# Input bias, maxima shift and setup of a fused convolution-attention-transformer kernel: who does them, and when

## The chip, the cores and the metric
One core of a Trainium2 chip runs the whole program. The metric is the device time of one execution in microseconds (us). Engines: PE (TensorE, matmul), PEld (its weight loads), DVE (VectorE), ACT (ScalarE), POOL (GpSimd), SP (SyncE, which here only issues DMAs). PE's clock has two levels, 1.2 and 2.4 GHz; the profile gives the granted one as 0.5 or 1.00.

## The reference
The input x has 32 images of 128 channels by 1024 pixels. For each image:

```
h    = group_norm(x)                                   # 32 groups of 4 channels
q,k,v = qkv_w @ h + qkv_b                              # over 1024 pixels
x1   = x + proj_w @ (v @ softmax(q^T k / sqrt(128))) + proj_b     # "global attention"
t    = x1 as 1024 tokens of 128
a    = window_attention(ln(t))                         # windows of 32 tokens, 8 heads of 16
m    = ln(ln(t) + a) * g1 + b1                         # transformer layer
m2   = ln(m + relu(m @ w1 + b1) @ w2 + b2) * g2 + b2
t2   = t + m2
out  = t2 + fp8_round(ln(t2)) @ fp8_round(kernel) + bias
```

Everything is fp32 in and out. The kernel writes most fp32 products as three products of 16-bit halves (high and low).

## The kernel before
An image passes through two stages. In the first (global attention) `gn0`, `gn1`, `gn2` make the group norm; `qg`, `kg`, `vg` project it (two halves of 512 columns each); 16 steps `max` multiply high halves of q and k and DVE takes each row's maximum (`cm`); `maxima` (line 684 on) reduces them per half to four maxima per partition, splits these into a bf16 high part and a rest in `cparts`; PE turns `cparts` (`shift`, line 914), DVE spreads the turned eight rows over [8 x 512] by a product with the selector `sel` (line 700), and each of the 16 score steps `st` starts its sum with one matmul of 512 columns, minus ones by this `shift` tile (line 927), before three products of halves. ACT takes the exponential, and `pv` multiplies by v, with the row sum in an extra column. `turn_x` transposes the image's own x on PE in two halves, and DVE adds proj_b as a row when it takes it out of PSUM into `xt` (line 678); `pv`'s last step adds that (line 716). In the second stage (two halves of 512 tokens each) come `ln_in`, `turn_in`, `k`, `q`, `v`, `score0/1`, `prob0/1`, `turn_p0/1`, `pv0/1`, `out`, `norm_mid`, `turn_mid`, `up0..3`, `down`, `norm_out`, `ln_q`, `quant`, `turn_q`, `ffn`.

The order of steps on each engine is written out by hand in `PROGRAM`: a word such as `max:5@4-` is step `max`, number 5, PSUM bank 4, of the image before this iteration's (one minus sign less or more is one image later or earlier). Each engine loops over the images in that order; steps wait for each other by semaphores, and a step that takes a PSUM bank also waits until its last tenant was read out. So PE has one fixed queue of work, and a late reader on DVE or ACT stops it.

Ahead of the loop stands a setup. SP issues the load of x and then 26 loads of weights and vectors that all count on one semaphore, `weights_in`. DVE waits for all of them (line 599), then makes halves of the weights and folds biases in a chain of 37 linked steps (`link`, each waiting for the last); PE waits for all 37 before the first projection. POOL makes constants, takes its part of the first group norm (`gn2`), and then clears three large tiles, `v32`, `kbd`, `ptbd`, with one memset each (line 367).

Of the kernel before, what the change touches and what calls it, by code (L numbers as in the profile page):

```python
# [25 lines left out]
P = 128  # L26
# [21 lines left out]
        max:1@0- vg:1@5- max:2@4- max:3@3- pv0:0@1-- max:4@2- max:5@4- turn_in:1@0-- pv1:0-- max:6@5- max:7@3-  # L48
        k:1@0-- out:0@4-- v:1@5-- max:8@0- q:1@3-- turn_x:0@2- shift:0@4- max:9@1- max:10@5- st:0@0- max:11@1-
        turn_mid:0@3-- pv:0- score0:1@4-- score1:1@2-- up0:0@0-- st:1@5- st:2@1- up1:0@3-- turn_x:1@4- max:12@5-  # L50
        up2:0@2-- up3:0@3-- pv:1- max:13@0- down:0@2-- st:3@0- max:14@3- max:15@5- pv0:1@1-- pv1:1-- pv:2- st:4@0-
        out:1@2-- st:5@5- st:6@0- pv:3- pv:4- gn1:0@0 shift:1@3- st:7@1- pv:5- turn_mid:1@3-- pv:6- pv:7- up0:1@2--
        up1:1@1-- up2:1@0-- up3:1@4-- st:8@3- down:1@5-- st:9@2- st:10@5- turn_in:0@2- pv:8- st:11@3- k:0@0- pv:9-
        st:12@2- q:0@1- pv:10- st:13@3- pv:11- st:14@2- gn2:0@3 turn_q:0@5-- st:15@3- pv:12- pv:13- score0:0@1-
        score1:0@0- v:0@2- pv:14- qg:0@4 kg:0@5 pv:15- vg:0@0 turn_q:1@2-- kg:1@3 qg:1@1 ffn:0@5-- max:0@5 ffn:1@2--""",
    "dve": """
        prob1:0-- kg:0- pv:15-- turn_p0:0-- ln_in:1-- qg:0- turn_p1:0-- max:0- kg:1- qg:1- max:1- max:2- max:3-
        max:4- max:5- turn_in:1-- max:6- pv1:0-- max:7- k:1-- out:0-- maxima:0- max:8- shift:0- max:9- q:1--
        turn_x:0- max:10- max:11- turn_mid:0-- score0:1-- score1:1-- prob0:1-- prob1:1-- turn_p0:1-- turn_x:1-
        turn_p1:1-- gn0:0 max:12- max:13- down:0-- max:14- max:15- pv1:1-- out:1-- maxima:1- shift:1- gn1:0  # L60
        turn_mid:1-- ln_q:0-- pv:7- ln_in:0- quant:0-- down:1-- turn_in:0- k:0- ln_q:1-- q:0- gn2:0 quant:1--
        score0:0- score1:0- prob0:0-""",
    "act": """
        vg:1- turn_in:1-- pv1:0-- k:1-- q:1-- v:1-- norm_mid:0-- st:0- turn_mid:0-- score0:1-- up0:0-- st:1-
        score1:1-- st:2- up1:0-- load_x:0 up2:0-- up3:0-- st:3- pv1:1-- st:4- norm_out:0-- st:5- st:6- norm_mid:1--
        st:7- turn_mid:1-- up0:1-- up1:1-- up2:1-- up3:1-- quant:0-- st:8- norm_in:0- st:9- turn_in:0- st:10-
        norm_out:1-- k:0- st:11- q:0- st:12- st:13- quant:1-- gn2:0 st:14- st:15- turn_q:0-- v:0- score0:0-
        score1:0- kg:0 turn_q:1-- qg:0 ffn:0-- qg:1 kg:1 vg:0 ffn:1-- norm_in:1-""",
    "pool": """
        prob1:0-- ln_in:1-- out:0-- norm_mid:0-- prob0:1-- prob1:1-- bias_out:1-- keep:0-- down:0-- out:1--  # L70
        norm_out:0-- norm_mid:1-- ln_q:0-- keep:1-- ln_in:0- quant:0-- down:1-- norm_out:1-- ln_q:1-- gn2:0
        quant:1-- prob0:0- bias_out:0-""",
# [72 lines left out]
def build(nc, a, out, images=IMAGES):  # L145
    ctx = ExitStack()
    with ctx:
# [23 lines left out]
        BO, RG1, RB1, RB2, RG2, RBL2, PROJR = range(7)  # L171
        rows = sb("rows", [P, 7, P])
# [6 lines left out]
        sel = sb("sel", [2 * HT, HT, P])  # L179
        minus1 = sb("minus1", [P, P], BF16)  # L180
# [19 lines left out]
        chi = sb("chi", [P, HT], BF16)  # L200
        cparts = sb("cparts", [P, P])
        shift = sb("shift", [P, 2, HT, P], BF16)
# [25 lines left out]
        wraw = xt[:].rearrange("p a b c -> p (a b) c")  # L228
        w1raw, kraw = e[:, 0, 0, :], et[:, 0, 0, 0:P]
        ones = p32[:, 0, 0:P]  # L230
        vb_full = p32[:, 1, 0:2 * P].rearrange("p (a b) -> p a b", b=P)
# [5 lines left out]
        def tiles(ap):  # L237
# [3 lines left out]
        s = {n: sem(n) for n in """weights_in const_made const_mask setup_dve setup_mm  # L241
            x_in gn_stats gn_mv gn_mm gn_mean gn_diff gn_var gn_veps gn_pow gn_scale gn_neg gn_coef h32_made h_hi h_lo
# [51 lines left out]
        def _(sp):  # L294
            def load(dst, src):
                sp.dma_start(dst, src).then_inc(s["weights_in"], 16)

            def prologue():
                sp.dma_start(x_sb[:, :], a["x"][0]).then_inc(s["x_in"], 16)
                load(wraw[:, QG:QG + 2, :].rearrange("p a b -> p (a b)"), a["qkv_w_t"][:, 0:2 * P])  # L300
                load(wraw[:, VG, :], a["v_w"])
                load(wraw[:, PROJ, :], a["proj_w_t"])
                load(wraw[:, Q:Q + 3, :].rearrange("p a b -> p (a b)"), a["in_w_t"])
                load(wraw[:, OUT, :], a["out_w_t"])
                load(w1raw, a["w1_t"])
                load(w2[:], a["w2_t"].rearrange("(t p) d -> p t d", p=P))
                load(kraw, a["kernel"])
                with nc.allow_non_contiguous_dma("short vectors, once"):
                    for at, width, name in ((QGB, 3, "qkv_b"), (PROJB, 1, "proj_b"), (GNW, 1, "gn_w"), (GNB, 1, "gn_b"),
                                            (QB, 3, "in_b"), (LN1B, 1, "ln1_b"), (FFNB, 1, "ffn_b"), (B1, FT, "b1"),  # L310
                                            (LN1G, 1, "ln1_g")):
                        load(cols[:, at:at + width], a[name].rearrange("(t p) -> p t", p=P))
                    load(col(S_IN), a["s_in"].partition_broadcast(P))
                    load(col(S_K), a["s_k"].partition_broadcast(P))
                for at, name in ((BO, "out_b"), (RG1, "ln1_g"), (RB1, "ln1_b"), (RB2, "b2"), (RG2, "ln2_g"),
                                 (RBL2, "ln2_b"), (PROJR, "proj_b")):
                    load(rows[:, at, :], a[name].partition_broadcast(P))
# [23 lines left out]
        def _(pool):  # L341
            g = nc.gpsimd

            def prologue():
# [10 lines left out]
                g.affine_select(out=sel[:], in_=sel[:], compare_op=ALU.not_equal, fill=1.0, base=0,  # L355
# [5 lines left out]
                g.affine_select(out=sel[:], in_=sel[:], compare_op=ALU.not_equal, fill=1.0, base=-HT,  # L361
                                pattern=[[-1, HT], [0, P]], channel_multiplier=1).then_inc(s["const_mask"], 1)
                for tile, value in ((cparts[:], 0.0), (minus1[:], -1.0), (vg32[:], 1.0), (ones, 1.0), (shift[:], 0.0)):
                    g.memset(tile, value).then_inc(s["const_made"], 1)
                gn2(None, 0, 0)
                for tile in (v32, kbd, ptbd):
                    g.memset(tile[:], 0.0).then_inc(s["const_made"], 1)
# [81 lines left out]
        def _(act):  # L449
# [22 lines left out]

            def normalise(dst, src, k):
# [20 lines left out]
            def vg(kind, img, c):  # L494
                act.wait_ge(s["vg_mm"], upto(img, c + 1, per=2))
                if isinstance(img, int) and img == 0 and c == 0:
                    act.wait_ge(s["const_made"], 10)
# [3 lines left out]
                sc.activation(vg32[:, HT * c:HT * (c + 1), 0:C], tiles(bank("vg", c)), ACT.Copy).then_inc(s["vg_made"], 1)  # L501

# [28 lines left out]
            def v(kind, img, h):  # L531
                n = 2 * img + h
                act.wait_ge(s["v_mm"], upto(n))
                if isinstance(img, int) and img == 0:
                    act.wait_ge(s["const_made"], 13)
# [31 lines left out]
            def ffn(kind, img, h):  # L567
# [3 lines left out]
                if due(value := upto(img - 1, step=16)):  # L571
# [6 lines left out]
                      "quant": normalise(z, u, 3), "load_x": load_x, "gn2": gn2, "qg": global_hi("qg", qgh, QGB), "kg": global_hi("kg", kgh, KGB), "vg": vg, "st": st,  # L578
# [7 lines left out]
        def _(dve):  # L586
# [9 lines left out]
            def prologue():  # L596
                gn0(None, 0, 0)
                dve.wait_ge(s["weights_in"], 16 * 26)
                dve.wait_ge(s["const_made"], 10)
                dve.wait_ge(s["const_mask"], 6)  # L600
# [500 lines left out]
```

## Time and profile before

| | us |
|---|---|
| median of 3 runs (lowest to highest) | 2459.72 (2457.88 to 2463.32) |
| the profiled execution | 2464.32 |
| its span, first to last instruction | 2462.6 |
| PE busy in the span | 2184.8 (89%) |
| DVE, ACT, POOL busy | 1878.0 (76%), 1380.6 (56%), 1224.1 (50%) |

The busy shares are means over the start, the steady loop and the end. A matmul's busy time in the profile contains its latency, so matmuls that follow each other overlap, and PE's share is not its share of peak.

### The profile page before, as it was taken

The numbers are of one execution on the slowest core, as the hardware profiler recorded it, in microseconds if no ns is written. First come the engines' busy times: TensorE is split into PE (matmuls) and PEld (weight loads), VectorE is DVE, ScalarE is ACT, GpSimd is POOL, SyncE is SP. The second block draws the span as 40 slices with busy tenths as digits, with TensorE's granted clock in tenths as the row PEclk, the third lists the DMA queues.
The fourth block names the chain that finished last, engine by engine and source line by source line (L and its number), as shares of the span: only waits on it lengthen the run. The fifth ranks groups of instructions, "written<-read, shape, count | busy, mean of one in ns | idle before, by whom it ended". The sixth has DMA issues, their size and how long they took to land.

```text
span 2462.6 us, 63216 instructions
## 1 busy us (share of the span) xinstructions
PE 2184.8 (89%) x21489; PEld 1606.4 (65%) x21710; DVE 1878.0 (76%) x5861; ACT 1380.6 (56%) x2721; POOL 1224.1 (50%) x1303
## 2 busy tenths in 40 slices
PE   1798899999999999999999999999999999999984
PEld 0566667766667766666776666676666677666663
DVE  5488777778777778887777888777887777788753
ACT  0355566555565555556655556665555655555653
POOL 5044455544455645455554545555544555444544
PEclk9999999999999999999999999999999999999997
DMA  1011111111101111110111111111111011111110
GB/s 34 14 31 44 43 28 38 26 38 43 43 26 39 27 40 38 43 43 26 38 26 40 41 43 38 30 38 26 38 43 43 26 38 26 41 40 43 29 31 19
DMA packets 76238, 86.15 MB, mean 35 GB/s; under 512 B 20640, under 2 KB 55584, under 8 KB 76192
## 3 DMA queue, kind: packets, MB, share of 16 engines
q1 hardware_dynamic: 62512, 52.51, 9.3%
q10 hardware_dynamic: 13680, 33.04, 3.9%
q8 instruction: 28, 0.46, 0.1%
q14 instruction: 18, 0.15, 0.0%
HBM read 18.36 MB, written 16.78 MB: 14 GB/s over the span
## 4 chain that ended last, share of the span: by engine, by line
PE 63%; DVE 11%; issue 6%; ACT 4%; DMA 4%; SPq 1%; ACTq 1%; POOL 1%; DVEq 0%; POOLq 0%
PE ps L944 16%; PE ps L851 9%; PE ps L852 8%; PE ps L853 8%; PE ps L1037 6%; PE ps L1006 5%; DMA x_sb<-in_x 3%; PE ps L911 3%; PE ps L988 3%; PE ps L954 2%; PE ps L927 2%; DVE cm L682 2%; DVE stats L723 1%; DVE y L794 1%; ACT o_sb L573 1%
## 5 line engine op out<-in xcount | busy, mean ns | idle before, releaser
L382 POOL TENSOR_TENSOR rstd<-veps,halfpow 128x4 f32<-128x4 f32 x256 | 266.7, 1042 | 816.0 <-DVE veps L731 814.9
L944 PEld LDWEIGHTS ps<-vg,p 128*128 128x128 f32 x4096 | 511.1, 192 | 49.0 <-issue 12.1
L944 PE MATMUL ps<-vg,p 128*128 128x129 f32 x4096 | 533.2, 277 | 0.6 <-ACT p L508 0.6
L508 ACT ACTIVATE p<-ps 128x512 f32<-128x512 f32 x512 | 294.4, 587 | 260.6 <-PE ps L853 260.6
L682 DVE TENSOR_REDUCE cm<-ps 128x1 f32<-128x512 f32 x512 | 330.4, 676 | 16.9 <-PE ps L911 16.7
L1037 PEld LDWEIGHTS ps<-w,hid 128*128 128x128 f32 x2048 | 235.2, 192 | 17.9 <-ACT hid L560 12.8
L1037 PE MATMUL ps<-w,hid 128*128 128x128 f32 x2048 | 242.3, 277 | 1.8 <-ACT hid L560 1.7
L851 PE MATMUL ps<-qgh,kgh 128*128 128x512 f16 x512 | 194.5, 380 | 42.9 <-DVE shift L700 19.9
L911 PE MATMUL ps<-kgh,qgh 128*128 128x512 f16 x512 | 173.9, 392 | 61.5 <-ACT vg L501 37.4
L560 ACT ACTIVATE hid<-ps,cols 128x512 f32<-128x512 f32 x256 | 170.7, 686 | 72.3 <-PE ps L853 72.3
L853 PE MATMUL ps<-qgh,kgl 128*128 128x512 f16 x512 | 194.5, 380 | 0.0
L852 PE MATMUL ps<-qgl,kgh 128*128 128x512 f16 x512 | 194.5, 380 | 0.0
L416 POOL TENSOR_TENSOR e<-e,srec 128x512 f32<-128x512 f32 x128 | 134.3, 1050 | 119.8 <-DVE srec L774 119.7
L482 ACT ACTIVATE y<-y,nshift,rstd 128x128 f32<-128x128 f32 x256 | 105.6, 483 | 77.6 <-POOL nshift L389 77.6
L1006 PE MATMUL ps<-ptbd,v 128*32 128x128 f32 x4096 | 137.0, 281 | 11.5 <-DMA ptbd<-et 11.5
L1006 PEld LDWEIGHTS ps<-ptbd,v 128*32 128x32 f32 x4096 | 109.8, 113 | 47.6 <-issue 29.0
L482 ACT ACTIVATE z<-u,nshift,rstd 128x128 f32<-128x128 f32 x256 | 105.1, 481 | 60.5 <-POOL nshift L389 60.5
L741 DVE TENSOR_TENSOR xl<-ps,xh 128x512 f16<-128x512 f32 x128 | 87.8, 686 | 62.0 <-ACT xh L516 59.5
L546 ACT ACTIVATE e<-e 128x512 f32<-128x512 f32 x128 | 80.6, 630 | 92.9 <-DVE e L764 92.9
L482 ACT ACTIVATE y<-t,nshift,rstd 128x128 f32<-128x128 f32 x256 | 105.5, 482 | 42.8 <-POOL nshift L389 24.0
L516 ACT ACTIVATE xh<-ps 128x512 f16<-128x512 f32 x128 | 76.4, 597 | 73.8 <-PE ps L954 73.8
L927 PE MATMUL ps<-shift,minus 128*128 128x512 bf16 x291 | 111.1, 382 | 5.0 <-DVE cm L682 4.8
(188 smaller groups left out, 5439.9 us busy)
## 6 DMA issues: line engine op xcount, KB each, us to landing
ptbd<-et SPq DMA_DIRECT2D x512, 64.0 KB, 2.0
kbd<-kk SPq DMA_DIRECT2D x512, 32.0 KB, 2.0
out_y<-o_sb ACTq DMA_DIRECT2D x64, 256.0 KB, 2.3
x_sb<-in_x ACTq DMA_DIRECT2D x31, 512.0 KB, 3.3
x_sb<-in_x SPq DMA_DIRECT2D x1, 512.0 KB, 3.5
e<-in_w_t SPq DMA_DIRECT2D x1, 256.0 KB, 3.6
w<-in_w_t SPq DMA_DIRECT2D x1, 256.0 KB, 3.4
xt<-in_in_w_t SPq DMA_DIRECT2D x1, 192.0 KB, 2.8
```

What stands on the lines that cost most here:

```text
L382: g.tensor_tensor(rstd[:, k, h, :], veps[:, k, h, :], halfpow[:], ALU.pow).then_inc(s[f"ln_pow{k}"], 1)
L482: last = sc.activation(dst[:, h, P * j:P * (j + 1)] if dst is z else dst[:, h, j, :], src[:, h, j, :], ACT.Identity, bias=nshift[:, k, h, ...
L508: sc.activation(p32[:, c % PRING, :], bank("st", c), ACT.Exp, scale=C ** -0.5).then_inc(s["p_made"], 1)
L560: sc.activation(hid[:, f, :], bank(f"up{f}", h), ACT.Relu, bias=col(B1F + f)).then_inc(s["hid_made"], 1)
L682: v_.reduce_max(cm[:, c // 2, c % 2:c % 2 + 1], bank("max", c), X).then_inc(s["max_out"], 1)
L851: mm(dst, lhi, rhi, start=first, stop=False, **kw)
L852: mm(dst, lhi, rlo, start=False, stop=False, **kw)
L853: return mm(dst, llo, rhi, start=False, stop=last, **kw)
L911: mm(bank("max", c), qgh[:, P * (c // 2):P * (c // 2 + 1)], kgh[:, HALF * (c % 2):HALF * (c % 2 + 1)], start=True, stop=True).then_inc(s[" ...
L944: last = mm(ps[:, b, at:at + PVW], p32[:, c % PRING, part], vg32[:, j, :], start=j == 0 and q % 2 == 0, stop=j == MT - 1, skip_group_check ...
L1006: last = mm(ps[WIN * two:WIN * (two + 1), BANK["pv0", h], P * j:P * (j + 1)], v32[:, h, odd, j, WIN * two:WIN * (two + 1)], ptbd[:, h, j, ...
L1037: last = mm(bank("down", h)[:, part], hid[:, f, part], w2[:, f, :], start=f == 0, stop=f == FT - 1)
```

## The change
Six edits, made together:

- turn_x: ACT adds proj_b to x_sb in place, per channel, in one step `bias_x`, after the group norm has read x; PE's transposes wait for it, and ACT, not DVE, copies them into `xt` (two copies of 512 columns). The folded bias of v (v's bias times proj_w) is a column now and not a row.
- shift: `cparts` is bf16, its transpose is a bf16 one, ACT, not DVE, copies the turned eight rows ([8 x 128]), and the spreading over 512 columns is done by PE: each `st` starts with four matmuls of 128 columns with four stationary tiles of a bf16 selector that holds -1. The separate tile `chi` is gone.
- the setup's loads: seven (qkv_w, v_w, proj_w, qkv_b, gn_w, gn_b, proj_b) come first on a semaphore of their own, `first_in`; the other 18 follow.
- the setup's DVE chain: seven steps come before the loop (halves of q's and k's weights, the product v times proj and its bias); the rest runs on DVE as the end of `maxima:0` of the first image, and PE's part at the end of its first `shift` step. The first `pv` waits for the steps that read PSUM, the first `turn_in` for all.
- POOL clears `v32`, `kbd`, `ptbd` in 26 pieces in place of three.
- `PROGRAM` is a new order on all engines, with other banks. Among others `out:0` and `gn0` come after `maxima` and no longer before it.

```diff
+        max:1@1- max:2@2- max:3@0- vg:1@5- turn_in:1@3-- pv0:0@1-- max:4@2- max:5@5- k:1@4-- max:6@0- pv1:0--
+        max:7@3- turn_x:0@4- v:1@5-- out:0@2-- q:1@1-- shift:0@0- turn_x:1@3- max:8@2- st:0@4- max:9@0- st:1@3-
...
-        for tile in (v32, kbd, ptbd):
-            g.memset(tile[:], 0.0).then_inc(s["const_made"], 1)
+        for h in range(2):
+            g.memset(v32[:, h], 0.0).then_inc(s["const_made"], 1)
+            for head in range(HEADS):
+                g.memset(kbd[:, h, head], 0.0).then_inc(s["const_made"], 1)
+            for j in range(HT):
+                g.memset(ptbd[:, h, j], 0.0).then_inc(s["const_made"], 1)
...
+    def bias_x(kind, img, _):
+        act.wait_ge(s["h32_made"], upto(img))
+        sc.activation(x_sb[:], x_sb[:], ACT.Identity, bias=col(PROJB)).then_inc(s["x_bias"], 1)
+    def turn_x(kind, img, c):
+        sc.activation(xt[:, c], tiles(bank("turn_x", c)), ACT.Copy).then_inc(s["xt_made"], 1)
+    def make_shift(kind, img, c):
+        sc.activation(shift[0:2 * HT, c, :], bank("shift", c)[0:2 * HT, 0:P // 2].bitcast(BF16),
+                      ACT.Copy).then_inc(s["shift_made"], 1)
...
     def prologue():                                    # DVE
         gn0(None, 0, 0)
-        dve.wait_ge(s["weights_in"], 16 * 26)
...
         gn1(None, 0, 0)
+        dve.wait_ge(s["first_in"], 16 * 7)
+        halves(QG)
+        halves(KG)
         gn2(None, 0, 0)
         dve.wait_ge(s["setup_mm"], 1)
...
+    def setup_rest():                                  # DVE, at the end of maxima:0 of image 0
+        dve.wait_ge(s["weights_in"], 16 * 18)
+        link(v_.tensor_scalar(vb_full, ones, col(VB), None, ALU.mult))
+        halves(Q)
+        halves(K)
+        dve.wait_ge(s["rest_mm"], 1)
...
     def st(kind, img, c):                              # PE
-        mm(bank("st", c), minus1[:], shift[:, h].rearrange("p a b -> p (a b)"), start=True, stop=False)
+        for q in range(HT):
+            mm(bank("st", c)[:, P * q:P * (q + 1)], sel[:, q, :], shift[:, h, :], start=q == 0, stop=False,
+               skip_group_check=True)
         three(bank("st", c), kgh[:, keys], kgl[:, keys], qgh[:, queries], qgl[:, queries],
-              first=False).then_inc(s["st_mm"], 1)
+              first=False, skip_group_check=True).then_inc(s["st_mm"], 1)
```

## Rows read from the trace of the kernel before

**Rows 1.** Windows: length, busy of PE, PEld, DVE, ACT, POOL, clock, DMA.
```profile
1354.50:1426.90 72.40, 67.22 (x673) 49.63 (x679) 57.65 (x182) 43.06 (x85) 37.47 (x41) 1.00 0.14 36
1358.70:1391.70 33.00, 28.53 (x328) 19.62 (x323) 31.45 (x76) 20.25 (x39) 15.57 (x15) 1.00 0.19 52
```
**Rows 2.** Timeline of PE, one iteration: start, length, idle before and releaser.
```profile
1354.56 0.28 PE L879 MATMUL ps<-gtmp,group_mean 128*128 128x1 f32 x2
...
1426.94 0.28 PE L879 MATMUL ps<-gtmp,group_mean 128*128 128x1 f32 x2
```
**Rows 3.** Waits of PE in that iteration: total, times, longest.
```profile
PE ps L917 <- DVE cparts L695: 1.3, 1, 1.3
PE ps L911 <- ACT vg L501: 1.2, 1, 1.2
PE ps L911 <- ACT o_sb L573: 0.8, 1, 0.8
PE ps L851 <- DVE shift L700: 0.6, 1, 0.6
```
**Rows 4.** Timeline of DVE in that iteration.
```profile
1377.10 0.68 DVE L794 TENSOR_TENSOR y<-ps,y 128x512 f32<-128x512 f32 x1
...
1379.28 0.15 DVE L687 TENSOR_REDUCE cmax<-cm 128x4 f32<-128x8 f32 x1
...
1392.71 0.69 DVE L639 BATCH_NORM_STATS2 gst<-x_sb 128x6 f32<-128x512 f32 x1 [1.00 <-DMA x_sb<-in_x]
```
**Rows 5.** Groups by form, 1000 to 2200 us: busy, mean ns, idle before.
```profile
L927 PEld LDWEIGHTS ps<-shift,minus 128*128 128x128 bf16 x261 | 26.1, 100 | 35.6 <-DVE cm L682 18.2 <-DVE w L805 6.6 <-DVE gtmp L655 2.9
...
L678 DVE TENSOR_TENSOR xt<-ps,rows 128x512 f32<-128x512 f32 x34 | 22.5, 661 | 0.0
L700 DVE TENSOR_TENSOR shift<-ps,sel 8x512 bf16<-8x512 f32 x33 | 22.2, 674 | 15.6 <-PE ps L917 15.6
...
L501 ACT ACTIVATE vg<-ps 128x512 f32<-128x512 f32 x34 | 20.0, 587 | 0.0
L461 ACT ACTIVATE hh<-x_sb,gtmp 128x1024 f16<-128x1024 f32 x16 | 19.6, 1227 | 0.0
```
**Rows 6.** Timeline of PE: a 512-column bf16 matmul.
```profile
1387.09 0.38 PE L927 MATMUL ps<-shift,minus 128*128 128x512 bf16 x1
```
**Rows 7.** Timeline: four 128-column bf16 matmuls, each with its own weights.
```profile
1001.93 0.39 PE L1046 MATMUL ps<-identh,qz 128*128 128x128 bf16 x4
```
**Rows 8.** Timeline of the start, all engines; SPq is SP's issue queue.
```profile
0.80 0.40 SPq L299 DMA_DIRECT2D x_sb<-in_x  x1
...
6.59 0.43 SPq L296 DMA_DIRECT2D cols<-in_gn_b  x1
...
18.30 0.28 DVE L601 TENSOR_SCALAR p<-p,cols 128x128 f32<-128x128 f32 x1 [12.44 <-DMA rows<-in_proj_b]
...
22.64 0.16 DVE L655 TENSOR_SCALAR gtmp<-ps 128x1 f32<-128x1 f32 x1 [3.08 <-PE ps L879]
...
27.57 1.80 POOL L367 MEMSET v<- 128x2048 f32 x1
27.81 15.33 DVE L607 CAST wh<-xt 128x128 f16<-128x128 f32 x1
29.32 13.75 POOL L367 MEMSET kbd<- 128x16384 f16 x1
...
43.50 6.58 DVE L607 CAST wh<-xt 128x128 f16<-128x128 f32 x1
50.12 0.29 DVE L608 TENSOR_TENSOR wl<-xt,wh 128x128 bf16<-128x128 f32 x1
...
58.81 0.10 PEld L851 LDWEIGHTS ps<-hh,wh 128*128 128x128 f16 x1 [36.30 <-DVE kl L635]
```
**Rows 9.** DMA issues: size, us to landing.
```profile
cols<-in_gn_b SPq DMA_DIRECT2D x1, 0.5 KB, 2.3
```
**Rows 10.** Timeline of PE in the loop's first full pass.
```profile
85.20 0.61 PE L927 MATMUL ps<-shift,minus 128*128 128x512 bf16 x1 [4.79 <-DVE cm L682]
```

## What was predicted before the changed kernel ran
> **What bounds the kernel now.** I read the busy line and the 40 slices first: PE is high in all slices but the first two and the last two. So there are two questions: what one iteration of the steady loop costs, and what the start costs. For the loop I took one iteration on PE's timeline, from one image's second group-norm matmul to the next: 1426.94 - 1354.56 = 72.4 us [rows 2]; 31 such iterations make 2244 us of 2462.6. In it PE is busy 67.2 us, DVE 57.7, ACT 43.1, POOL 37.5 [rows 1], so PE bounds the loop and what can be won is its waits. The view of waits names them [rows 3]: 1.3 us for `cparts` before the transpose of the maxima, 1.2 and 0.8 at the loop's end where `max` waits for ACT's read-out, 0.6 for `shift`; with three smaller ones 4.8 us in all. They lie in or beside a stretch of 33.0 us in which DVE is busy for 31.45 [rows 1]: there DVE, not PE, sets the pace. So DVE work is dear inside this stretch and nearly free outside it. For the start the timeline says it plainly: the first projection's weights load at 58.81, after a wait of 36.3 us for the last step of DVE's chain [rows 8]. That chain waited to 18.30 for the last of 26 loads, and two of its casts took 15.33 and 6.58 us, each ending as one of POOL's large memsets does.
>
> **The start.** Issues lie (6.59 - 0.80)/12 = 0.48 us apart [rows 8], so the seventh load after x goes out at 0.8 + 7 x 0.48 = 4.2, and with 2.3 us to landing [rows 9] `first_in` is full at 6.5 (qkv_b has three columns: 7). The group norm's first half, which needs only x, is through by then. PE makes two small products and the second group-norm matmul, about 1.6 us, to 8.7. From that matmul's reader to POOL's first large memset, which starts as the low half of the normed image is made, are 27.57 - 22.64 = 4.9 us [rows 8]: 13.6. The seven DVE steps (two pairs in front of it, three behind) hide in this. So the first projection starts at about 14 in place of 58.8: **45 us earlier**, 40 if a load or a lock adds five.
>
> Not all of it stays. The rest of DVE's chain moves behind `maxima:0` of image 0. Before, from 50.12 to 58.8 [rows 8], the chain's free-running end took 8.6 us, for the same number of steps within three. Behind it on DVE stand `max:8` and all later maxima, and PE waits for their banks; PE has some 3 us of its own there (`turn_x:1`, two `st`, two `max`), so 8.6 - 3 = 5.6 us return. POOL cleared from 27.57 to the end of the second long cast at 50.08 [rows 8], 22.5 us; in 26 pieces it does so from 14 to 37, and in this time (the rest of the chain starts near 28) DVE's casts meet them. If a cast waits for one piece, half a piece of 0.87 is 0.4 us for each of about 12: +4, of which the last few fall after 37. If it doesn't get in between pieces (the cast of 27.81 outlasted the 1.80 us memset of `v` and ended with that of `kbd` at 43.1 [rows 8]), it stands until 37: +9. I take +4. The first full pass also had a 4.79 us wait of PE [rows 10]: DVE stood in `gn0` for the next x with two `max` behind it. `gn0` moves behind `maxima:1`, so this goes: -4. Sum of the start: -45 + 5.6 + 4 - 4 = -39, rounded down to **-37** for steps I can't see (bounds -28 and -44).
>
> The Trainium skill (SBUF — State Buffer, section on ports) says that the pair of ports which VectorE and GpSimd share is locked for a whole instruction. The trace agrees in that the casts end with memsets, not in that a boundary between two memsets was enough; by the rule taken to the letter pieces cost half a piece each, which is the +4 I took.
>
> **The loop, DVE and ACT.** DVE loses two `turn_x` of 661 ns, two `shift` of 674 ns [rows 5] and two small copies, 3.0 us an iteration; three of the four large ones and one copy, 2.2 us, lie in the crowded stretch. `out:0` stood before `maxima:0` and held it for 1379.28 - 1377.10 = 2.2 us [rows 4]; now it is behind. So `cparts` comes about 3 to 4 us earlier relative to the `max` steps, more than the 1.3 us that PE waits there. The `shift` link shrinks from a 674 ns DVE step queued behind a `max` to a small ACT copy of about 0.25. `gn0`'s 1.00 us wait for its DMA [rows 4] leaves the front of `max:12` too. ACT gains one [128 x 1024] Identity, 1.23 us as `hh`, two copies of 587 ns [rows 5] and two small ones: +2.9 us, to 46 of 70. Its steps that PE waits for soon (`turn_q`, `o_sb`, `kgh`, `vg`) aren't behind `bias_x`; `k:1` is, and had its result needed only six steps later.
>
> **The loop, PE.** One 512-column matmul (0.38 us busy, [rows 6]) becomes four of 128 with their own weights; four such in a row are busy 0.39 [rows 7]. So +0.01 x 16 = 0.2 us at most, and a bf16 transpose in place of an fp32 one gives back about 0.1. I take zero (bounds -0.1 and +0.3 an iteration).
>
> **The loop, the order.** I added up step durations along PE's new queue and looked at each wait by hand. Waits I still find: about 0.4 at `ffn:1` for `turn_q`, 1.4 at `max:1` (its bank is released by DVE's `qg:1`, which stands behind `ln_in`, two transposes and `qg:0`), 0.6 at `turn_mid:0`, and 1.4 in crumbs. Gone are the two for the maxima (1.3 + 0.6), the `ol` one, and half of that at the loop's end: up to 2.8 us won. Each hand-over I left out goes against this, so I take two thirds, **-1.8 us an iteration** (bounds: -3.2 and, as any order can hide a new wait of a DMA or a POOL step, +0.3), x 31 = **-56 us**. The end (the last image's second stage) I take as unchanged, +-4.
>
> **Sum.** The profiled execution took 2464.3; 2464.3 - 37 - 56 = 2371. The median of the runs lies 4.6 lower at 2459.7, from which the same sum gives 2367. I say **2369**.
>
> **Rivals.**
> 1. Only the start gains. The PE waits at the loop's end are of ACT and DVE order, not of load, and a new order can trade 1.9 us of one wait for others: iteration 72.4 as before, time 2460 - 37 = 2423. For it: each wait in [rows 3] is at most 1.3 us, about what one step placed two places too early brings back. Against: 2.2 us of DVE work leaves a stretch that has only 1.5 us of slack.
> 2. Slower by ACT. The 2.9 us land in front of `p`, and `pv` on PE waits for it; no more than four `p` tiles are open. If all of it shows, 31 x 2.9 = +90, less the start's 37: 2513. It decides from +1.2 us an iteration on. For it: `norm_mid` and `st` share that stretch of ACT. Against: ACT is busy 43 of 72, and 20 of 33 in the stretch [rows 1].
> 3. Slower by weight loads. Of four loads of 100 ns [rows 5] three are new; were they in the open between short matmuls, 0.3 x 16 x 32 = +154, less 37: 2577. Against: [rows 7]. The Trainium skill (TensorE: Matmul & The Clock Gate, "Back-to-back issue gap") speaks for a milder form: 81 ns for each 128-column matmul in a stream of load and matmul pairs and 131 for a 512-column one, by which 16 x 32 x (324 - 131) ns = +99 us; the trace has neither figure, its 128-column ones being spaced as [rows 7] shows.
> 4. The start gives less, because DVE's chain stands behind POOL's pieces until 37 and `v`'s or `kbd`'s readers wait too: start -28, time 2378 with the loop as forecast.
>
> **How the numbers follow.** Loop and start both gain: 0.72 (rival 4 is in it). Only the start: 0.17. ACT 0.05, weight loads 0.03; 0.03 for a loop that loses just what the start wins. The likeliest case itself spans 2464 - 44 - 99 = 2321 to 2423. To hold 8 in 10 the range leaves out the far low end and takes in rival 1: 2328 to 2430. With about 0.2% (5 us) as what can be told from no change: faster 0.90, same 0.02, slower 0.08.
>
> **What would show it.** First projection near 14, and DVE's chain after `maxima:0` about 10 us long with PE waiting some 6 to 10 in it. An iteration of 70.6 between second group-norm matmuls; no PE wait for `cparts` or `shift`; the 128-column selector matmuls spaced so that `st` stays near 0.86 us; the 4.79 wait gone. DVE 54.7 and ACT 46 busy an iteration. Wrong if an iteration is 72 or more, or if the largest PE wait names an ACT step behind `bias_x`, or DMA-fed `pv0`/`pv1`.

## The result, and the profile after

| | before | changed |
|---|---|---|
| median of four runs, us | 2460.10 (2457.88 to 2463.32) | 2379.01 (2369.09 to 2409.28) |
| ratio | | 0.966, 95% interval 0.961 to 0.971 |
| span of the profiled execution | 2462.6 | 2407.5 |
| to the second group-norm matmul of image 1 | 115.2 | 77.2 |
| from there to that of image 31, 30 passes | 2184.0 | 2172.4 |
| from there to the end | 163.4 | 157.9 |

The time lies 10 us from the forecast of 2369, with the sign as forecast. The runs of the changed kernel spread over 40 us, those of before over 5; the profiled one is the slowest of the four, so by their times it holds more of the long passes told below than the other three. The ratio leaves this run out, since its 2409.28 lies more than 1.5% above the fastest of its kernel.

**A pass as it should be.** The windows of the changed kernel show one iteration (length, busy of PE, PEld, DVE, ACT, POOL, clock, DMA share, GB/s), then one of 80 us:

```profile
1115.84:1185.54 69.70, 67.82 (x729) 51.49 (x728) 54.19 (x177) 45.60 (x90) 37.55 (x41) 1.00 0.14 38
291.12:371.06 79.94, 70.56 (x729) 53.24 (x727) 54.52 (x177) 45.65 (x90) 37.61 (x40) 0.94 0.13 35
```

The first row answers to [rows 1]: 69.7 us for 72.4, DVE 54.2 busy (57.7 before), ACT 45.6 (43.1 before). PE's waits in seven such passes (1046 to 1534 us; total, times, longest), all that the view lists:

```profile
PE ps L938 <- DVE qgl L704: 9.0, 7, 1.3
PE ps L929 <- DVE kk L779: 1.6, 7, 0.2
PE ps L1092 <- ACT qt L586: 1.1, 7, 0.2
```

Of the four waits of [rows 3] none is there: `cparts`, `vg`, `o_sb` and `shift` hold PE no more. One of 1.3 us stands in their place, at `max:1`. All waits together are 11.7 / 7 = 1.7 us a pass, against 4.8.

**Eight passes that aren't.** Of the 30 passes between the two matmuls 22 take 69.7 to 71.7 us, and eight take 78 to 80. PE's timeline at the end of one of them (start, length, idle before):

```profile
304.54 0.38 PE L938 MATMUL ps<-kgh,qgh 128*128 128x512 f16 x1
309.06 1.44 PE L938 MATMUL ps<-kgh,qgh 128*128 128x512 f16 x3 [4.14 <-issue]
...
312.27 0.27 PE L877 MATMUL ps<-wh,hl 128*128 128x128 f16 x1 [1.24 <-issue]
```

The releaser is "issue": the profile shows nothing that PE waited for. What PE's queue did in that time is one instruction, the branch at the loop's end. Its group in the changed kernel (line, queue, operation: ns min/median/max, first and last start), and the queue of instruction loads of that pass, then of the whole span (packets, MB, share):

```profile
L285 PEldq COMPARE_BRANCH  x28: 76/213/4896, 304.2 to 2261.8; - x28
```
```profile
q8 instruction: 9, 0.15, 0.8%
```
```profile
q8 instruction: 102, 1.67, 0.3%
```

The branch takes 0.21 us in 20 passes and 4.4 to 4.9 us in eight, the eight of 78 to 80 us. Before, the longest was 0.24 us and the queue moved 28 packets in all; now each of the eight has nine packets of 16 KB and a clean one has none. The two idle stretches, 4.14 and 1.24, are half of the 79.9 - 69.7 = 10.2 us by which this pass is longer. Most of the other half is the clock, in the windows around it:

```profile
304.10:309.10 5.00, 0.86 (x11) 0.53 (x8) 3.15 (x6) 2.82 (x6) 0.54 (x2) 0.76 0.40 109
309.10:319.00 9.90, 8.66 (x90) 5.28 (x90) 4.96 (x8) 3.00 (x5) 2.50 (x2) 0.61 0.13 31
```

PE stood for 4.1 us, and in the 10 us after it the granted clock was 0.61: most of them at 1.2 GHz. By an estimate this costs 9.9 x (1 - 0.61) = 3.9 us. Behind the other seven long branches the 10 us show 0.54 to 0.68.

**The start.** DVE and PE around the first projection and the first maxima:

```profile
13.47 0.27 PE L875 MATMUL ps<-wh,hh 128*128 128x128 f16 x1 [5.33 <-POOL hl L380]
```
```profile
26.40 10.17 DVE L720 CAST cparts<-cmax 128x4 bf16<-128x4 f32 x1
```
```profile
36.91 0.27 PE L944 MATMUL ps<-identh,cparts 128*128 128x128 bf16 x1 [12.03 <-DVE cparts L722]
...
47.65 0.61 PE L938 MATMUL ps<-kgh,qgh 128*128 128x512 f16 x1 [3.39 <-DVE cm L710]
```

The first projection runs at 13.47 in place of 58.8 [rows 8]. But the cast of four numbers per partition, the first DVE instruction of its kind after POOL began to clear, takes 10.17 us: it ends at 36.57, as POOL's last piece does (36.5). While PE waits for it, the granted clock falls, by the window from 30 to 40 us to 0.50:

```profile
30.00:40.00 10.00, 3.09 (x15) 3.12 (x16) 8.45 (x9) 0.27 (x1) 6.54 (x8) 0.50 0.00 0
```

From 40 to 50 us it is 0.67, and PE's 512-column matmuls of that time take up to 0.63 us in place of 0.38. The prediction's sum of the start has no term for the clock.

### The profile page after: what moved, and what is told of

It reads as the page before. It is cut to its first block, busy times and chain, and to the rows that moved or that the text cites. A ratio compares the mean times of both kernels' runs of the same rounds, so it can differ in the third digit from the quotient of the medians.

```text
span 2407.5 us, 66541 instructions
## 1 busy us (share of the span) xinstructions
PE 2210.5 (92%) x23246; PEld 1672.1 (69%) x23246; DVE 1757.0 (73%) x5668; ACT 1461.4 (61%) x2881; POOL 1229.0 (51%) x1325
## 3 DMA queue, kind: packets, MB, share of 16 engines
q8 instruction: 102, 1.67, 0.3%
## 4 chain that ended last, share of the span: by engine, by line
PE 66%; DVE 10%; issue 8%; ACT 6%; DMA 5%; SPq 4%; POOL 1%; ACTq 0%; DVEq 0%; POOLq 0%
PE ps L977 15%; PE ps L875 8%; PE ps L1072 8%; PE ps L877 7%; PE ps L876 7%; PE ps L1041 4%; PE ps L957 4%; PE ps L938 4%; DMA ptbd<-et 3%; PE ps L1023 3%; PE ps L989 3%; SPq L323 2%; DMA kbd<-kk 2%; SPq L330 1%; ACT y L498 1%
## 5 line engine op out<-in xcount | busy, mean ns | idle before, releaser
L977 PEld LDWEIGHTS ps<-vg,p 128*128 128x128 f32 x4096 | 503.5, 192 | 37.6 <-ACT p L529 4.6
L977 PE MATMUL ps<-vg,p 128*128 128x129 f32 x4096 | 520.6, 277 | 0.7 <-ACT p L529 0.7
L710 DVE TENSOR_REDUCE cm<-ps 128x1 f32<-128x512 f32 x512 | 335.9, 681 | 40.4 <-PE ps L938 40.2
L938 PE MATMUL ps<-kgh,qgh 128*128 128x512 f16 x512 | 183.2, 398 | 69.4 <-issue 34.8
L581 ACT ACTIVATE hid<-ps,cols 128x512 f32<-128x512 f32 x256 | 165.7, 684 | 96.3 <-PE ps L877 96.3
L957 PE MATMUL ps<-shift,sel 128*128 128x128 bf16 x2048 | 198.6, 220 | 0.0
L957 PEld LDWEIGHTS ps<-shift,sel 128*128 128x128 bf16 x2048 | 155.4, 98 | 56.7 <-ACT hid L581 2.1
L403 POOL TENSOR_TENSOR y<-y,rows 128x512 f32<-128x512 f32 x64 | 81.5, 1273 | 172.2 <-PE ps L989 172.2
L572 ACT ACTIVATE oh<-ps 128x512 f16<-128x512 f32 x64 | 38.2, 597 | 186.9 <-PE ps L1041 186.9
L938 PEld LDWEIGHTS ps<-kgh,qgh 128*128 128x128 f16 x512 | 49.3, 98 | 143.8 <-issue 99.3
```

What stands on the lines that cost most here:

```text
L581: sc.activation(hid[:, f, :], bank(f"up{f}", h), ACT.Relu, bias=col(B1F + f)).then_inc(s["hid_made"], 1)
L710: v_.reduce_max(cm[:, c // 2, c % 2:c % 2 + 1], bank("max", c), X).then_inc(s["max_out"], 1)
L938: mm(bank("max", c), qgh[:, P * (c // 2):P * (c // 2 + 1)], kgh[:, HALF * (c % 2):HALF * (c % 2 + 1)], start=True, stop=True).then_inc(s[" ...
L957: mm(bank("st", c)[:, P * q:P * (q + 1)], sel[:, q, :], shift[:, h, :], start=q == 0, stop=False, skip_group_check=True)
L977: last = mm(ps[:, b, at:at + PVW], p32[:, c % PRING, part], vg32[:, j, :], start=j == 0 and q % 2 == 0, stop=j == MT - 1, skip_group_check ...
```

## The experiments

**What makes the long passes.** PE's part of the loop grew from 1483 to 1581 instructions, counted in the traces (the trace of before shows 1476, with 671 matmuls for 678 weight loads; before_moves below, which has the same steps, shows all 1483). My theory was that none of its steps is slow, and that where the loop lies decides whether its first instructions are still held at the branch. The rivals: the number of instructions, or the short weight loads.

`pad32` and `pad96`: the changed kernel with 32 or 96 PE instructions ahead of the loop that wait for something long done.

```diff
             def prologue():
+                for _ in range(N):             # and as many behind gn2; two waits make one instruction
+                    pe.wait_ge(s["const_made"], 1)
                 gn1(None, 0, 0)
```

> The changed kernel with 32 more PE instructions ahead of the loop (waits that are already met), nothing else. In the changed kernel's trace PE's branch at the loop's end takes 0.21 us in 20 of 28 passes and 4.4 to 4.9 us in 8, and exactly in those passes the instruction queue moves nine packets of 16 KB; the passes last 78 to 80 us in place of 69.7. Theory (instruction fetch): PE's loop of 1581 instructions covers seven blocks of 256 and ends near a block's end; what was kept of the loop is lost when fetching runs past it. Counted from where the packets fall ahead of the loop, 32 more instructions make it span eight blocks: all 28 branches slow, some 250 instruction packets, time near 2330 + 28 x 9 = 2580 us, slower than the kernel before. Rival A (clock): the slow passes come from PE's clock alone, set off by the waits in the order: 0 to 10 slow passes as now, 2370 to 2410 us. Rival B: random DMA contention: the same.

> The same with 96 such instructions: by the instruction-fetch theory the loop then spans seven blocks and ends 80 instructions into its last: no slow branch, some 28 instruction packets, every pass 69.7 us, time 2367.3 less its slow passes, near 2335 us (the 96 waits cost up to 3 at the start). Rival A and B: 2370 to 2410 us with up to 10 slow passes, as the changed kernel.

Measured: pad32 2334.89 (2334.17 to 2335.68), ratio 0.947 (0.945 to 0.949); pad96 2330.62 (2326.78 to 2333.53), 0.945 (0.943 to 0.948). Neither has a long branch. pad96:

```profile
L285 PEldq COMPARE_BRANCH  x28: 76/208/234, 301.4 to 2183.8; - x28
```
```profile
q8 instruction: 30, 0.49, 0.1%
```

So position decides, and rivals A and B are out. Some 48 us (2379.0 - 2330.6; by the two ratios 2.0%, 50 us) come back with instructions that do nothing. But my count of blocks, by which 32 would make all passes slow, was wrong.

`one512`: the changed kernel with one 512-column selector matmul that reads the 128-column shift four times over; 1485 PE instructions in the loop. This kernel leaves out a part of the computation: three of the four query tiles of a half are shifted by the maxima of another tile and not by their own.

```diff
-                for q in range(HT):
-                    mm(bank("st", c)[:, P * q:P * (q + 1)], sel[:, q, :], shift[:, h, :], start=q == 0, stop=False, ...)
+                mm(bank("st", c), sel[:, 0, :], shift[:, h:h + 1, :].to_broadcast([P, HT, P]), start=True, stop=False, ...)
```

> The changed kernel with one matmul of 512 columns ahead of each score step in place of four of 128 (the shift tile read four times over; the shift subtracted is then that of another query tile, so this part of the computation is changed). PE's loop body is 96 instructions shorter. Theory: four short matmuls cost what one long one does (0 to +0.3 us a pass), and the loop no longer ends near a block's end: no slow branch, 69.4 to 69.7 us a pass, 2325 to 2340 us. Rival A (clock): slow passes stay, 2370 to 2410. The rival of the prediction by weight loads (81 ns for each short matmul): a pass shorter by 3 us, 2240.

Measured: 2326.84 (2324.02 to 2329.52), ratio 0.944 (0.942 to 0.946), no long branch, pass 69.63 against 69.70. The 48 additional matmuls and their loads cost 0.07 us a pass, where the rival by weight loads had 3.

`before_split`: the opposite direction. The kernel before, its 512-column matmul cut in four with the same minus ones; 1579 PE instructions in the loop (its trace shows 1575 to 1583 in a pass, that of split_pad 1579 in each).

```diff
-                mm(bank("st", c), minus1[:], shift[:, h].rearrange("p a b -> p (a b)"), start=True, stop=False)
+                for q in range(HT):
+                    mm(bank("st", c)[:, P * q:P * (q + 1)], minus1[:], shift[:, h, q, :], start=q == 0, stop=False, ...)
```

> The kernel before with each 512-column matmul of minus ones cut into four of 128 columns, nothing else: 96 more PE instructions in the loop (1572). Theory: 72.4 to 72.7 us a pass; the loop spans seven blocks and ends 56 instructions ahead of its last block's end, so few or no slow branches: 2460 to 2470 us. If the mere number of instructions is what counts, slow passes come as in the changed kernel: 2490 to 2540. Rival (weight loads): +3 us a pass, 2550.

Measured: 2578.97 (2563.93 to 2592.35), ratio 1.048 (1.043 to 1.053), where I expected few or no long branches: the count of blocks failed here too. Most clean passes stay at 72.4 to 72.6; 11 of 28 branches take 5.0 to 5.9 us and their passes 80 to 82.

```profile
L287 PEldq COMPARE_BRANCH  x28: 76/222/5919, 353.5 to 2410.7; - x28
```
```profile
q8 instruction: 129, 2.11, 0.4%
```

The fault is carried into a kernel that hadn't it, without one step of the change's order. `split_pad` then takes it away from there: before_split with 96 instructions of padding.

> The kernel before with its 512-column matmul cut in four (before_split, 2578.97, with 11 long branches of 28), and besides 96 PE instructions that wait for nothing ahead of the loop. If what makes the long branches is where the loop lies among the instructions, and not how many it has (1575 in both), they are gone: no branch over 0.3 us, about 28 instruction packets, every pass 72.4 to 72.5 us, and 2462 to 2472 us. If the number of instructions in the loop is what counts, the time stays at 2560 to 2590 with 10 or so long branches.

Measured: 2469.18 (2463.74 to 2476.33), ratio 1.002 (1.001 to 1.004), no long branch.

```profile
L287 PEldq COMPARE_BRANCH  x28: 76/208/246, 352.3 to 2318.3; - x28
```

The same loop with the same 1579 instructions, 110 us apart: it is the position, shown in both directions. It also prices the weight loads in the kernel before: cut and padding cost 6 us together, of which 3.0 lie ahead of the second group-norm matmul of image 1 and 3.4 in the 30 passes behind it, 0.1 a pass. Which positions are bad stays half open. Counted along the trace, good to two or three, the first branch is PE's instruction 5578 in the changed kernel and 5563 in before_split, 202 and 187 modulo 256. In the kernels without long branches the rest is 25 (split_pad), 42 (pad96 and the runs built on it), 57 (before_moves, with the PE steps of before), 74 (one512, yield_one) and 234 (pad32). Why only 8 to 11 of 28 branches are long stays open too. The Trainium skill (Runtime: NRT & Kernel Launch, "Instruction fetch mechanics") says that PE's instructions are refilled in 16 KiB blocks of 256, and that a taken branch whose target isn't held forces a fetch before execution goes on. The packets of 1.67 MB / 102 = 16.4 KB and the branches of 4.9 us agree. That the same loop is held or not by its position, and in one pass of three, the section doesn't say.

**What the start is worth.** All on pad96, against its 2330.6, since no long pass covers a few us there.

`bigmem`: three large clears again in place of 26 pieces.

```diff
-                for h in range(2):
-                    g.memset(v32[:, h], 0.0)...          # and 8 pieces of kbd, 4 of ptbd
+                for tile in (v32, kbd, ptbd):
+                    g.memset(tile[:], 0.0).then_inc(s["const_made"], 1)
```

> The same base, with POOL's 26 clears put back into three. In the base DVE's four-element cast of the maxima stands from 26.7 to 36.9, through 12 pieces, until POOL's last one ends. Theory (DVE doesn't get in between pieces, so pieces are worth nothing): the cast waits until a clear ends and DVE gets in at 29 or at 36.6 as before: start the same within 1 us or up to 1 us shorter, 2330. Rival (pieces help): start 2 to 5 us longer, 2335.

Measured: 2329.06 (2327.42 to 2330.22), ratio 0.945 (0.944 to 0.947). The pieces are worth nothing. The cast of bigmem beside its clears, then that of pad96 beside its own:

```profile
15.31 13.75 POOL L366 MEMSET kbd<- 128x16384 f16 x1
29.00 6.92 POOL L366 MEMSET ptbd<- 128x8192 f32 x1
```
```profile
26.86 9.08 DVE L716 CAST cparts<-cmax 128x4 bf16<-128x4 f32 x1
```
```profile
25.19 0.95 POOL L366 MEMSET v<- 128x1024 f32 x1
26.08 7.21 POOL L368 MEMSET kbd<- 128x1024 f16 x8
33.23 3.64 POOL L370 MEMSET ptbd<- 128x1024 f32 x4
```
```profile
26.71 10.19 DVE L720 CAST cparts<-cmax 128x4 bf16<-128x4 f32 x1
```

The cast of bigmem ends at 35.94 with the 6.92 us clear, passing over the boundary at 29.0; that of pad96 passes over eleven. In these two runs no boundary between two clears that stand in POOL's queue one behind the other lets the waiting cast in; in the kernel before, one of two did (see the part on the prediction).

`yield`: POOL stops after 13 pieces until the setup's chain is through.

```diff
                 for h in range(2):
+                    if h:
+                        pool.wait_ge(s["setup_dve"], SETUP_STEPS)
                     g.memset(v32[:, h], 0.0).then_inc(s["const_made"], 1)
```

> The same base, POOL clears the first 13 pieces (to 25.2 us) and waits for DVE's setup chain before the other 13. Theory (the 10.2 us of the cast are POOL's clears): the cast takes 0.2, DVE's chain ends near 37 in place of 47, and PE's first pass is 8 to 10 us shorter: 2321. Rival (the cast's length has another cause, or the later clears stop something else by the same time): 2331.

Measured: 2320.17 (2318.68 to 2320.51), ratio 0.941 (0.940 to 0.943). DVE and POOL in yield:

```profile
28.14 0.17 DVE L722 CAST cparts<-cmax 128x4 bf16<-128x4 f32 x1
```
```profile
22.12 3.64 POOL L372 MEMSET ptbd<- 128x1024 f32 x4
37.65 0.95 POOL L368 MEMSET v<- 128x1024 f32 x1 [11.88 <-DVE kl L669]
```

With POOL idle the same cast takes 0.17 us, and 10.4 us of the total go, about what the cast stood; 8.6 of them lie ahead of the second group-norm matmul of image 1 (68.9 for 77.6).

`onechain`: the chain's second part back in front of the loop on DVE and PE, loads and pieces as changed.

```diff
                 link(v_.tensor_tensor(col(PROJB), ps[:, 7, FT:FT + 1], col(PROJB), ALU.add))
+                setup_rest()
...
-                if isinstance(img, int) and img == 0 and c == 0:
-                    setup_rest()
```

> pad96 (2330.6 us) with all of DVE's and PE's setup steps in front of the loop again, not at the end of the first maxima; the two-part loads, the early casts of q's and k's weights and POOL's 26 pieces stay. My theory: the gain of the start comes of the first projection that no longer waits for the chain. Then the first projection waits for the last of 25 loads (about 15 us), the two setup products and a chain of some 9 us which begins before POOL's clears: it starts at 24 to 32 us in place of 13.8, PE's stop behind maxima:0 (some 12 us) goes in return, and so the time is only 2 to 12 us longer, 2333 to 2343. If one of the chain's casts is caught by POOL's pieces again, as in the kernel before, the projection waits to about 45 to 50 us and the time is 2350 to 2360. Rival: moving the chain is worth nothing, because its length comes back whole behind maxima:0 and what won was only the early end of the waiting for the loads: 2328 to 2333.

Measured: 2337.18 (2324.37 to 2339.78), ratio 0.947 (0.944 to 0.951). The first projection comes at 37.56, 24 us later than in pad96, since again one DVE step stood for POOL:

```profile
17.87 19.04 DVE L639 TENSOR_SCALAR res<-res,cols 128x128 f32<-128x128 f32 x1 [6.23 <-DMA rows<-in_ln_b]
```

It costs 6.6 us by the medians, inside my 2333 to 2343, though the first projection came in neither of my two windows, and the intervals of the two ratios overlap. In the traces the second group-norm matmul of image 1 comes 8.4 us later (85.9 for 77.6). So of the 37.7 us that the start gained to this matmul, the chain's new place gives some 8, although it moves the first projection by 24: PE's 12.0 us wait behind `maxima:0` is 1.6 here. The larger part comes of what this kernel keeps. I put it down to the loads in two parts, which is argued: no run has all loads on one semaphore again. Without the two parts gn2, and with it POOL's clears, had to wait for 26 loads; POOL was through at 50.1 [rows 8] and is at 36.9 here, and DVE's chain ends 13 us earlier (58.8, here 45.4) though undivided. The step is a TENSOR_SCALAR, so casts aren't the only kind that stands.

**What the loop is worth.** `turnx_dve`: pad96 with the two copies of `turn_x` on DVE as before, put behind `maxima:0` and `max:8`.

```diff
-        max:6- pv1:0-- max:7- maxima:0- out:0-- max:8- max:9-            # DVE's order
+        max:6- pv1:0-- max:7- maxima:0- turn_x:0- out:0-- max:8- turn_x:1- max:9-
```

> The same base, with the two turn_x copies back on DVE (two steps of 0.66 us, put behind maxima:0 and max:8), the bias left on ACT. Theory of the prediction (work on DVE in the crowded stretch is dear): 1.2 us more in that stretch, of which PE has to wait some 0.6 to 1.2: 70.3 to 70.9 a pass, 2350 to 2368. Rival (the gain of the loop came from the new order, not from the load): +0 to 0.2 us a pass, 2331 to 2337.

Measured: 2399.85 (2394.63 to 2422.35), ratio 0.973 (0.971 to 0.974). That is over my 2350 to 2368. A clean pass is 71.63, +1.9, more than the 1.3 us that the two copies take. PE's waits, 1100 to 1600 us:

```profile
PE ps L946 <- DVE qgl L704: 11.4, 7, 2.4
PE ps L965 <- DVE xt L710: 9.2, 7, 1.3
```

In a clean pass `st` now waits 1.3 us for a bank that DVE's copy gives back, `max:1` waits its 1.3 as before, and small ones (`y` of DVE and of ACT, 0.2 each) make up the rest. DVE work near the crowded stretch comes through whole and more.

Nine of the 30 passes take 73 to 76 us besides. In each of the nine, and in no other of the 30, one DVE step of 0.43 us in `quant` stands beside POOL's `hl`:

```profile
524.39 2.13 POOL L380 TENSOR_TENSOR hl<-h,hh 128x1024 f16<-128x1024 f32 x1 [2.31 <-ACT hh L464]
524.39 2.41 DVE L850 TENSOR_SCALAR expo<-expo 128x512 f32<-128x512 f32 x1
```

Here the two start within 0.02 us of each other in nearly every pass. If POOL is first, DVE's step takes 2.4 us and `max:1` waits 2.4; if DVE is first, its step takes 0.43 and `hl` 2.4. In pad96 DVE is 0.05 us or more ahead wherever the two meet, and its step always takes 0.43. So the two copies also moved DVE to the edge of a collision with POOL, and a part of the 69 us (2399.9 - 2330.6) is that.

`before_moves`: the opposite, the order without the load. The kernel before with `out:0` behind `maxima:0` and `gn0` behind `maxima:1` on DVE.

```diff
-        ... k:1-- out:0-- maxima:0- max:8- ...   gn0:0 max:12- ...   maxima:1- shift:1- gn1:0
+        ... k:1-- maxima:0- out:0-- max:8- ...   max:12- ...   maxima:1- gn0:0 shift:1- gn1:0
```

> The kernel before with two moves in DVE's order alone: out:0 behind maxima:0, gn0 behind maxima:1. If the order near the maxima makes up much of the changed kernel's 2.7 us a pass, this alone gives 0.3 to 1.0 us a pass and takes the 4.79 us wait of the first pass away: 2425 to 2450. If what won is DVE's lighter load, and the order only moves waits between steps, the pass stays within 0.3 us of 72.4 and the time is 2450 to 2468.

Measured: 2501.45 (2498.77 to 2504.66), ratio 1.016 (1.014 to 1.018): slower, which neither of my cases had. The pass is 73.6, +1.2. PE's waits, 1100 to 1600 us, of before_moves:

```profile
PE ps L927 <- DVE shift L700: 8.5, 7, 1.2
PE ps L911 <- ACT vg L501: 6.9, 6, 1.2
PE ps L874 <- DVE gmv L643: 5.9, 7, 0.8
PE ps L911 <- ACT o_sb L573: 4.7, 6, 0.8
PE ps L954 <- ACT y L482: 4.3, 7, 0.6
PE ps L911 <- ACT v L540: 4.0, 7, 0.6
```

The wait for `cparts` (1.3 a pass, [rows 3]) is gone as meant. In its place stand `shift` with 1.2 (0.6 before), `gmv` with 0.8, since `gn0` and `gn1` now come late for the group norm, and `y` and `v` with 0.6 each. Only the start gained (gn2 of image 1 at 111.3, the 4.79 us wait gone). So the two moves that I had priced as gains don't pay in the old order. Whether they do in the new one, with the lighter DVE, no run shows by itself.

`swap`: pad96 with the banks of `max:1` and `max:2` exchanged, against the one large wait left.

```diff
-        max:1@1- max:2@2- max:3@0-
+        max:1@2- max:2@1- max:3@0-
```

> The changed kernel with 96 more PE instructions ahead of the loop (as run before: no slow pass, 69.7 us a pass, 2330.6), and banks 1 and 2 exchanged between max:1 and max:2. In each pass PE waits 1.3 to 1.6 us at max:1, whose bank is read out by DVE's qg:1; bank 2 is released by qg:0, one DVE step of 0.65 earlier. Theory (this wait is set by DVE's queue, and nothing close behind it): 69.1 us a pass, 31 x 0.6 = 19 less, 2312. Rival (the next wait takes it over: vg:1 needs bank 5 from DVE's max:0, pv0 its DMA): no change, 2331.

Measured: 2332.93 (2331.74 to 2333.57), ratio 0.947 (0.945 to 0.948), pass 69.79: no gain. PE's waits in it, 1100 to 1600 us:

```profile
PE ps L942 <- DVE qgl L704: 4.9, 14, 0.5
PE ps L993 <- ACT y L498: 2.2, 7, 0.3
...
PE ps L1045 <- DVE cm L710: 1.1, 5, 0.2
```

1.3 us at one place have become 0.7 at two together, 0.3 for `y` and 0.15 for `cm`. The bank only moves the wait; my reading is that DVE's pace sets it, which this run fits and doesn't prove.

**The fastest version.** `yield_one`: the changed kernel with yield's wait and one512's matmul, without padding. It leaves out what one512 leaves out, the own maxima of three tiles in four; of the versions that compute everything yield is the fastest.

> The changed kernel with the two things that won apart: POOL stops its clears after 13 pieces until the setup's chain is done (yield, 2320.2 on the padded kernel), and one 512-column matmul for the shift in place of four of 128 (one512, 2326.8 against 2330.6). No added PE instructions: with 1485 in the loop it lies where one512 and the kernel before have no long branches. If the gains add: 2313 to 2319. If they don't, because the 3.8 us of one512 came of something in the start which yield removes too: about 2320.

Measured: 2317.49 (2315.68 to 2319.87), ratio 0.941 (0.939 to 0.942): 62 us below the changed kernel, 3 below yield, though their ratios (0.9405 and 0.9413) can't be told apart.

## Why the prediction was near, and where it was wrong

The forecast was 2369; with the long passes taken out the changed kernel is 2330.6 (pad96). So 2379 lies close to the forecast because two errors cancel: I gave the loop and the end too little by some 40 us (2369 - 2330.6), and didn't foresee a fault that costs about 48. That the number came out near is luck. By the spans, pad96 against before (2328.2, 2462.6):

| | forecast | pad96 | changed kernel's profile |
|---|---|---|---|
| start (to gn2 of image 1) | -37 | -37.7 | -38.0 |
| loop | -56 | -89.9 | -11.6 |
| end | 0 | -6.8 | -5.5 |

- **The start** came out as summed, by terms that were not. The first projection at 13.5 to 13.8 was right (14). "Half a piece for each of about 12 casts: +4" failed: the bound beside it, a cast that stands until 37, is what happened, by one cast (to 36.6). Behind it the chain's second part took 10.3 us, as said; PE waited 12.0 + 3.4 = 15.4 us, where I had 5.6 + 4. The 4.79 us wait is gone, as said. -45.3 + 15.4 - 4.8 = -34.7, and most of the rest to -38 is the shorter pass, 2.7 us, which stood in the loop's term. The low clock behind the 12.0 us wait, for which I had nothing, is within these numbers and not told apart.
- **My reading of the pair of ports** was the mistake in this. In [rows 8] the first long cast passes over the boundary at 29.3 and ends at 43.14, just behind the boundary between `kbd` and `ptbd`, whose clear stands in the same trace:

```profile
43.01 7.00 POOL L367 MEMSET ptbd<- 128x8192 f32 x1
```

  So one boundary in two had let a cast in, and I took the price by which every one does. In bigmem, pad96 and onechain no boundary let the waiting step in, and it ended with POOL's last clear; in yield, with POOL idle, it ran at once. What decides at which boundary DVE gets in stays open. The Trainium skill (SBUF — State Buffer, "Who interferes with whom") has the lock for the whole of one instruction; that a step waits through twelve of them, as the cast of pad96 does, the section doesn't say. It says also that `cast` and `tensor_scalar` can take the shared pair and `tensor_reduce` never; there the trace agrees, as the stalled steps are a CAST and a TENSOR_SCALAR, and the TENSOR_REDUCE at 26.51 of pad96, 0.2 us ahead of the cast and under the same clear, took its 0.16 us.
- **The loop** was right in its mechanism and too small: 72.4 - 69.7 = 2.7 us a pass, where I had written 2.8 and taken two thirds of it. The mis-sized term is the third that I took off for hand-overs left out. The 2.8 itself doesn't follow from the waits listed beside it: those called gone add to 1.3 + 0.6 + 0.4 + 1.0 = 3.3, and those still found to 3.8 of the 4.8, which leaves 1.0; that it came out near 2.7 is no merit of the sum. The waits that I said would go went, the one named at `max:1` stands with 1.3 (I had 1.4), `turn_q` with 0.16 (0.4), `turn_mid` has none (0.6). DVE 54.2 and ACT 45.6 busy answer to 54.7 and 46. How the 2.7 divides stays open: with the two copies back on DVE 0.8 of it is left (72.4 to 71.6), two moves of the order in the kernel before lose 1.2, and no run has the lighter DVE in the old order.
- **The matmuls**: a step `st` is 0.87 us and the shift's four matmuls 0.39; one512 gives 0.07 us a pass for them, against 4.8 by rival 3 and 16 x 193 ns = 3.1 by its milder form, the 81 and 131 ns of the Trainium skill (TensorE: Matmul & The Clock Gate, "Back-to-back issue gap"). Both are dead in this kernel; rival 2 (ACT) too, as no wait of PE names a step behind `bias_x`.
- **Rival 1** (only the start gains) is what the span of this profile nearly shows, -11.6 us over 30 passes, and yet its mechanism, waits traded for waits, wasn't there. Who reads only the sums would have taken it as right.
- **What I left out**: I counted what PE does with 48 more matmuls and 48 more loads a pass, and not what the loop's length does to its instruction supply. The trace of before had a row for it, the 28 packets of instructions against 28 branches of 0.2 us, but nothing in it that could have told on which side of the edge the new loop would fall.

## What to carry to other kernels

When a hardware loop gets longer, look first at the loop-end branch of the engine that bounds and at the packets of the instruction queue: 96 idle instructions ahead of the loop were worth 48 us here, more than the start's 38. Don't clear large tiles on POOL while DVE has a critical chain, and don't count on the boundaries between pieces: make POOL wait. If single passes of a loop are longer than the others, compare the lengths of their steps with those of a clean pass: in turnx_dve a start a few hundredths of a us behind POOL's cost 3 us. In an order written by hand, price DVE work by the stretch that it lies in, and don't price a move by the wait that it removes alone.

## What the runs showed of the hardware

- PE's loop-end branch takes 0.21 us or 4.4 to 5.9 us, the latter with nine 16 KB instruction packets and, in the changed kernel, a granted clock of 0.54 to 0.68 in the 10 us after; in 8 (changed kernel) or 11 (before_split) of 28 passes, and in none with 96 instructions more ahead of the loop.
- A DVE cast of 4 elements per partition waited 10.19 us through 12 back-to-back POOL memsets, a TENSOR_SCALAR 19.04 us; with POOL idle the cast takes 0.17 us. In the kernel before, a cast ended at a boundary between two memsets (43.0 us) after it had passed over one (29.3).
- In turnx_dve a DVE TENSOR_SCALAR and a POOL TENSOR_TENSOR that start within 0.02 us of each other take 2.41 and 2.13 us with POOL first, 0.43 and 2.41 us with DVE first.
- Four 128-column bf16 matmuls with their own weights in place of one of 512 columns: 0.07 us for 16 of them a pass in the changed kernel, 0.1 in the kernel before.
